# Decoder layer with experts: first expert prepared in the routing block, GpSimd constants, ringed list buffers, 4 KB norm pieces

## The reference

```
probs = softmax(x @ Wr + br);  gates, ids = top_k(probs, 2)
# each expert takes the cap = ceil(1.2 * 8192 / 8) = 1229 tokens with the highest gates
xg = x[disp_tok]                                   # (8, cap, 256)
h = silu(xg @ W1 + b1);  out = h @ W2 + b2         # hidden width 1024
y = zeros.at[disp_tok].add(out * disp_g)
x = layernorm(x + y)
```

## Time and profile before

| what | us |
|---|---|
| median of 3 runs (lowest, highest) | 1637.54 (1636.06, 1637.61) |
| the profiled execution, its own time | 1637.37 |
| its span, first to last instruction | 1635.6 |
| routing block, 970.2 to 1097.6 | 127.4 |
| experts block up to its first product, 1097.6 to 1105.4 | 7.8 |
| norm block, 1586.4 to 1635.6 | 49.2 |

### The profile page before, as it was taken

The page is one execution under the profiler, slowest core; times in us unless marked ns, Lnnn a source line. Parts: engine busy times, 40 slices in busy tenths (PEclk is TensorE's granted clock), DMA queues, the critical chain, the costliest instruction groups (busy, mean ns, idle before and its releaser), DMA issues. The chain is left out here.

```text
span 1635.6 us, 43777 instructions
## 1 busy us (share of the span) xinstructions
PE 1412.0 (86%) x17886; PEld 1188.3 (73%) x17886; DVE 1021.5 (62%) x2276; ACT 1015.4 (62%) x1555; POOL 598.8 (37%) x607
## 2 busy tenths in 40 slices
PE   7999999999999999999998560119999999999940
PEld 5777777777777777777776340119999999999940
DVE  5666666666777777777777368955455445445425
ACT  4677777777777777777766352337555456556407
POOL 2645454544433232323230000032455445545236
PEclk9999999999999999999999885559999999999975
DMA  6112122221212222222221451013443444343139
GB/s 189 33 49 62 58 61 60 60 60 60 61 60 73 79 80 78 80 67 82 70 69 45 139 165 15 1 44 82 95 104 47 97 94 95 53 99 48 22 78 355
DMA packets 128006, 129.53 MB, mean 79 GB/s; under 512 B 26496, under 2 KB 114672, under 8 KB 127808
## 3 DMA queue, kind: packets, MB, share of 16 engines
q1 hardware_dynamic: 112704, 106.24, 21.3%
q0 software_dynamic: 15104, 20.48, 7.7%
HBM read 82.53 MB, written 44.16 MB: 77 GB/s over the span
## 5 line engine op out<-in xcount | busy, mean ns | idle before, releaser
L515 ACT ACTIVATE at_pr<-at_A 128x2048 f32<-128x2048 f32 x128 | 240.7, 1880 | 147.2 <-PE at_A L335 147.2
L610 DVE TENSOR_REDUCE at_mx<-at_A 128x12 f32<-128x1536 f32 x128 | 224.6, 1754 | 56.3 <-PE at_A L300 52.7
L35 PE MATMUL ex_D<-ex_w,ex_hT 128*128 128x256 f32 (+1 forms) x1920 | 234.2, 282 | 0.3
L35 PEld LDWEIGHTS ex_D<-ex_w,ex_hT 128*128 128x128 f32 (+1 forms) x1920 | 231.0, 184 | 2.9 <-DVE ex_raw L1582 1.8
L35 PE MATMUL ex_U<-ex_xT,ex_w 128*128 128x384 f32 (+1 forms) x1152 | 224.6, 354 | 3.4 <-DVE ex_xT L1559 3.4
L1639 POOL DMA_INDIRECT total<-ex_o,ids x80 | 131.4, 1642 | 237.1 <-DVE ex_o L1587 220.1
L35 PEld LDWEIGHTS ex_U<-ex_xT,ex_w 128*128 128x128 f32 x1152 | 208.4, 190 | 12.1 <-issue 3.8
L755 POOL TENSOR_SCALAR_AFFINE_SELECT at_pr<-at_pr 128x2048 f32<-128x2048 f32 x64 | 128.5, 2007 | 205.2 <-ACT at_pr L515 205.1
L1572 DVE TENSOR_TENSOR ex_hT<-ex_h,ex_hT 128x384 fp32r<-128x384 f32 (+1 forms) x192 | 112.6, 587 | 100.2 <-ACT ex_hT L1532 90.8
L646 DVE TENSOR_TENSOR at_oT<-at_C,at_oT 128x512 fp32r<-128x512 f32 x64 | 44.2, 691 | 165.3 <-ACT at_oT L528 165.3
L335 PE MATMUL at_A<-at_qp,at_kt 32*128 32x256 f32 x2048 | 139.8, 388 | 0.0
(11 more groups left out here) (219 smaller groups left out, 2690.1 us busy)
## 6 DMA issues: line engine op xcount, KB each, us to landing
w_in<-in_w SPq DMA_DIRECT2D x16, 1024.0 KB
at_turned<-in_x_turned SPq DMA_DIRECT2D x16, 512.0 KB, 4.6
at_x<-in_x SPq DMA_DIRECT2D x16, 512.0 KB, 4.1
x<-at_y SPq DMA_DIRECT2D x32, 256.0 KB, 2.4
at_x<-x SPq DMA_DIRECT2D x16, 512.0 KB, 3.8
at_turned<-in_ctx_turned SPq DMA_DIRECT2D x16, 512.0 KB, 4.8
rows<-at_y SPq DMA_DIRECT2D x32, 256.0 KB, 2.2
total<-at_y SPq DMA_DIRECT2D x32, 256.0 KB, 3.0
```

What stands on the lines that cost most here:

```text
L35: last = nc.tensor.matmul(out, pick_l(left, a), pick_r(right, b), start=(start and n == 0), stop=(stop and n == 2))
L515: nc.scalar.activation(pr[:, k % 2].rearrange("p i n a q -> p (i n a q)"), A[:].rearrange("p i n a q -> p (i n a q)"), ACT.Exp).then_inc(e ...
L610: nc.vector.tensor_reduce(mx[:, k % 2, 0:12], A[:, 0:3].rearrange("p i n a k -> p (i n a) k"), AX, ALU.max).then_inc(max_done, 1)
```

## The change

- The shared buffers of the two blocks (inputs and rounded parts of expert 0's weights, small inputs, gathered rows, `xT`, `gate`, `ident`, the two transpose banks) are made before both.
- SP loads expert 0's small inputs in the routing block, behind its weights; the experts block's own loads of them and of `ident` go.
- ACT rounds expert 0's weights between the exponential and `low`, and chunk 0's transposes at its block end. DVE takes the weights' rests right behind `ids`, then the gates of chunk 0 and the rests of `xT`. PE transposes chunk 0 at the end of the block.
- POOL gathers two chunks (six DMAs) in the routing block; the third chunk (four) is the first thing in the experts block.
- The memsets of DVE's opening go to POOL; PE waits for them ahead of the search, DVE ahead of `gt`. `base` is no longer cleared there and `ahead` no longer copied.
- The list tables are a ring of four batches; from the fifth batch on DVE waits for the PE products of four batches earlier.
- In the norm block a partition takes four neighbouring tokens: one piece of 4 KB a load and a store.

```diff
 # route_block: ACT
             nc.scalar.activation(warm[:], dummy[:], ACT.Sign)
+            act.wait_ge(sh["w_in"], 32)
+            for src, dst, _ in weights:
+                nc.scalar.copy(dst[:, 0], src[:]).then_inc(sh["w_hi"], 1)
             act.wait_ge(split, 1)
...
+            for half in range(HALVES):
+                act.wait_ge(sh["t_full"], half + 1)
+                nc.scalar.copy(xT[:, 0, 0, half, :widths[0]], T[half][:, 0:widths[0]]).then_inc(sh["x_hi"], 1)
 # route_block: PE
             last.then_inc(pe_done, 1)
+            pe.wait_ge(cleared, 1)
             for i in range(STEPS):
...
+            pe.wait_ge(x_loaded[0], 16 * parts[0])
+            for half in range(HALVES):
+                for k, (off, n) in enumerate(tiles_of[0]):
+                    last = nc.tensor.matmul(T[half][:, off:off + n], xg[0:n, 0, k, half * P:(half + 1) * P], ident[0:n, 0:n],
+                                            start=True, stop=True, is_transpose=True)
+                last.then_inc(sh["t_full"], 1)
 # route_block: DVE
-            v.memset(xg[:, :, parts[-1] - 1, :], 0.0).then_inc(cleared, 1)
-            v.memset(ones[:], 1.0)
-            v.memset(base[:], 0.0)
-            v.memset(ones_h[:], 1.0)
-            for i in range(STEPS):
-                for j in range(3):
-                    ins = v.memset(third[:, i, j:j + 1], (j + 1) * step_of(i) - half_unit(i))
...
             dve.wait_ge(pe_done, 1)
+            dve.wait_ge(cleared, 1)
...
+                at = b % RING
+                if b >= RING:
+                    dve.wait_ge(batch_done, b - RING + 1)
...
+            for k, (src, dst, _) in enumerate(weights):
+                dve.wait_ge(sh["w_hi"], k + 1)
+                v.tensor_tensor(dst[:, 1], src[:], dst[:, 0].bitcast(FP32), ALU.subtract).then_inc(sh["w_lo"], 1)
+            dve.wait_ge(sh["small_in"], 48)
+            dve.wait_ge(x_loaded[0], 16 * parts[0])
...
 # route_block: POOL
+            nc.gpsimd.memset(ones_h[:], 1.0)
+            for i in range(STEPS):
+                for j in range(3):
+                    nc.gpsimd.memset(third[:, i, j:j + 1], (j + 1) * step_of(i) - half_unit(i))
+            for j in range(3):
+                nc.gpsimd.memset(tries[:, j:j + 1], (j + 1) * step_of(0) - half_unit(0))
+            nc.gpsimd.memset(ones[:], 1.0)
+            nc.gpsimd.memset(xg[:, :, parts[-1] - 1, :], 0.0).then_inc(cleared, 1)
             pool.wait_ge(cleared, 1)
             pool.wait_ge(gates_stored, 16)
             pool.wait_ge(ids_made, 1)
-            for s in range(AHEAD):
+            for s in range(ROUTED):
 # experts_block: POOL
+            for s in range(ROUTED, AHEAD):
+                gather(s)
 # norm_block
-                             sum_dram[g * G:(g + 1) * G, :].rearrange("(b p) n -> p b n", p=P)).then_inc(loaded[g], 16)
+                             sum_dram[g * G:(g + 1) * G, :].rearrange("(p b) n -> p b n", p=P)).then_inc(loaded[g], 16)
```

More of the change, by code:

```diff
@@ L959, in _, with route_block @@
             take(groups - 1)
-def route_block(nc, tiles, cap, logits, rows_dram, ids, first_weights, first_rows, consts):
+def route_block(nc, tiles, cap, logits, rows_dram, ids, sh, consts):
     LT = -(-cap // P)
@@ L970, in route_block @@
     PARTS = tiles // BATCH
+    _, parts, starts, widths, tiles_of = chunks_of(cap)
     DVE_TAGS = 4
+    RING = 4
     Q = 2 * tiles
@@ L1043, in route_block @@
         empty = sb("empty", [P, ROWS])
-        w1_in, w2_in, w_in = first_weights
-        xg, x_loaded = first_rows
+        xg, x_loaded, xT, chosen, gate, ident, T = (sh[name] for name in ("xg", "x_loaded", "xT", "chosen", "gate", "ident", "T"))
+        weights = ((sh["w1_in"], sh["w1"][0], "w1"), (sh["w2_in"], sh["w2"][0], "w2"))
         cleared = sem("cleared")
@@ L1092, in _ @@
                 act.wait_ge(rows_hit, b + 1)
[L1093 to L1095 removed]
+                for k in range(BATCH):
+                    t = part * BATCH + k
+                    ins = nc.scalar.activation(tagged[:, b % RING, k, :], hit_row[:, b % RING, k, :], ACT.Copy, scale=tag[:, t:t + 1])
                 ins.then_inc(tags_made, 1)
+            for half in range(HALVES):
+                act.wait_ge(sh["t_full"], half + 1)
+                nc.scalar.copy(xT[:, 0, 0, half, :widths[0]], T[half][:, 0:widths[0]]).then_inc(sh["x_hi"], 1)
         @block.tensor
@@ L1125, in _ @@
                     pe.wait_ge(dve_tags, (b + 1) // DVE_TAGS)
[L1126 to L1131, removed]
+                for k in range(BATCH):
+                    last = nc.tensor.matmul(bi[:, part, :], hit_lane[:, b % RING, k, :], tagged[:, b % RING, k, :],
+                                            start=(b % 2 == 0 and k == 0), stop=(b % 2 == 1 and k == BATCH - 1))
+                last.then_inc(batch_done, 1)
+            pe.wait_ge(x_loaded[0], 16 * parts[0])
[4 more added lines that the diff above has]
+                last.then_inc(sh["t_full"], 1)
         @block.vector
@@ L1310, in chunks_of, with shared_by_route_and_experts, sb, sem @@
     return NC, parts, starts, widths, tiles_of
-def experts_block(nc, cap, rows_dram, ids, first_weights, first_rows, sum_dram, w, consts):
+def shared_by_route_and_experts(nc, c, cap):
+    _, _, _, widths, _ = chunks_of(cap)
+    W = max(widths)
+    def sb(name, shape, dt=FP32):
+        return c.enter_context(nc.sbuf_tensor("ex_" + name, shape, dt))
+    def sem(name):
+        return c.enter_context(nc.semaphore("ex_" + name))
+    sh = {name: sem(name) for name in ("w_in", "ident_in", "small_in", "t_full", "x_hi", "x_lo", "gate_ready", "chosen_ready",
+                                       "w_hi", "w_lo")}
+    sh["x_loaded"] = [sem(f"x_loaded{i}") for i in range(XG)]
+    sh["w1_in"] = sb("w1_in", [P, HALVES, HID])
+    sh["w2_in"] = sb("w2_in", [P, HT, D])
+    sh["w1"] = [sb("w1_even", [P, 2, HALVES, HID], FP32R)]
+    sh["w2"] = [sb("w2_even", [P, 2, HT, D], FP32R)]
+    sh["b1"] = sb("b1", [P, 2, HT])
+    sh["b2"] = sb("b2", [P, 2, D])
+    sh["mask"] = sb("mask", [P, 2, E])
+    sh["xg"] = sb("xg", [P, XG, NB, D + E])
+    sh["xT"] = sb("xT", [P, 2, 2, HALVES, W], FP32R)
+    sh["chosen"] = sb("chosen", [P, NB, E])
+    sh["gate"] = sb("gate", [P, NC_CHUNKS, NB])
+    sh["ident"] = sb("ident", [P, P])
+    sh["T"] = [c.enter_context(nc.psum_tensor(f"ex_T{i}", [P, G], FP32)) for i in range(2)]
+    return sh
+def experts_block(nc, cap, rows_dram, ids, sh, sum_dram, w, consts):
     LT = -(-cap // P)
```

104 lines of the change are left out of this document (42 added, 62 removed).

## The result

The changed kernel takes 1621.92 us (median of four runs, 1621.30 to 1623.79), against 1636.80 us (1636.03 to 1637.61) before: ratio 0.9911, 95% interval 0.9894 to 0.9928. Forecast were 1622.3 us. The profiled execution took 1622.32 us, its span 1620.3 (before 1637.37 and 1635.6). What follows takes that span apart, since 15.3 us of difference that agree with 15.1 us of forecast may still be made of other parts.

A forecast was written before the change was run, and what follows sets the result against it. PE bounds the middle stage; around it, PE's waits up to its first product and DMA in the norm block were taken to bound. 11.0 + 4.1 = 15.1 us off 1637.37 gives 1622.3; range 1619.3 to 1626.8.

The forecast's parts named there:

- Parts 1 to 3: Routing block: memsets moved to POOL, weights rounded early on ACT, and the ring of list tables each change nothing, cost 0.
- Part 4: End of routing block: PE's first product moves from 1105.4 to 1094.4, gain 11.0 us, bounds 8.8 and 12.8.
- The stall of 1.7 us: End of routing block: DVE's rests of the weights hold up POOL's first two gathers, 1.7 us, bounds 0 and 4.0.
- Part 5: Experts block: third chunk's gathers start late but land before PE wants them, cost 0, 1.8 us to spare.
- Part 6: Norm block, bound by DMA: 4 KB pieces at 404 GB/s take 45.1 us, gain 4.1 us.
- the cap by ACT: Norm block: ACT's last activation plus one 512 KB store would end it at 44.1 us, capping the gain at 5.1.
- the rival built on it: Norm block: 4 KB pieces move no faster, leaving only the route's gain, 1626.4 us; chance 0.14.
- The sum: Whole kernel: 11.0 us at the routing block's end plus 4.1 in the norm block, 15.1 us off 1637.37.
- The slow rival: Routing block: small memsets on POOL at 1.04 us each delay PE's search, 31.4 us more, 1653.7; chance 0.02.

The follow-up runs named there:

- no rests: Changed kernel without DVE's two subtractions for expert 0's weights, ACT writing a plain copy in their place: 1622.01 us, ratio 0.9908.
- one chunk routed: Changed kernel with only the first chunk's three gathers in the routing block, in place of two chunks: 1624.00 us, ratio 0.9924.
- three chunks routed: Changed kernel with all ten gathers of the first three chunks in the routing block, in place of six: 1627.12 us, ratio 0.9938.

## Why the prediction was right, point by point

- *Parts 1 to 3, nothing*: right. From exponential to list it is 104.48 us in the changed kernel, 104.47 before, and 104.57 with the memsets on DVE. The margins were real: POOL was done 18 us early, ACT 5 us early, and DVE's ring waits show nowhere (PE's product of batch 4 still waits 0.98 us for DVE's tagging, as in the earlier trace rows). The ring by itself was not tried.
- *Part 4, 11.0 us*: right at 11.3, for the reasons given. The stall of 1.7 us was 1.67 (no rests), POOL came last and not DVE (one chunk routed), four gathers were worth 5.26 of the 5.28 us counted (three chunks routed). The gathers went 2.36 and 1.60 us where I had drawn 2.1 and 2.0, with nearly the same sum. The first ended 1.2 us behind DVE's first operation (about 1081.6), the second 0.9 us behind its last at 1083.80. Both are 0.1 us under the length of a free gather at that place (1.32 and 1.01 us), as if nearly all of the gather came behind the hold. The Trainium skill, "SBUF — State Buffer", section "SBUF: two separate sides", has 0.115 us behind DVE's end for the hold; for the end of the gather the measurement decides.
- *Part 5, nothing*: right. PE does not wait for chunk 2's gathers in either profile of the changed kernel, and gathering it early gains nothing. What the forecast did not look at is that the load of expert 1's weights moves with these gathers, into the us in which ACT's gaps cost PE 1.2 us in the first profile.
- *Part 6, 4.1 us*: the right mechanism, mis-sized. The rate was 412 GB/s over both directions (413 in the first us, 420 towards the end), not 404: 40.7 us for the data in place of 41.5. The median block of 43.8 us leaves 3.1 us for start and landing, not 3.6. It is also the 44.1 us of the cap by ACT that I had worked out and not taken: ACT's last activation plus 3.6 to 4.3 us in eight of twelve profiles. DMA is still full then, so the cap is met by both together. The gain is 5.3 us as a rule (49.1 to 43.8), and 3.6 in the profiled execution, whose last DMAs trickled for two us more. The Trainium skill, "DMA: Bandwidth & Descriptors", section "Specifications", has line rate from 512 B on; here 1 KB pieces ran at 366 GB/s and 4 KB ones at 412, so the rival built on it fell.
- *The sum*: 15.1 forecast, 15.3 between the spans, but part of that agreement is luck. The first 1.7 us come from code ahead of the change: the routing block starts anywhere from 968.2 to 971.5 us in these fourteen profiles. The loss of 1.2 us in the experts block was not forecast and comes and goes with the chip or the execution; that the load's new place has no part in it is not shown. Without both the profile says 11.3 + 3.6 = 14.9, and with a norm block of the usual kind 16.6; the two series of runs said 14.9 and 16.8.
- *The slow rival*, memsets of 1.04 us on POOL: off by a factor of thirty. 45 of them took 1.55 us.

## What to carry to other kernels

When a block ends with an engine's queue of DMAs, count that queue and the others apart, each with its own way out (2.5 us behind an indirect gather here, 0.5 behind DVE), and move work out of the later one until both meet; beyond that the other one decides. Look also at what waits for the work that was moved: here a weight load went with the gathers. Large DVE operations with two inputs belong into the gaps where DVE waits for PE, not beside POOL's gathers, and POOL's large operations not beside DVE's with two inputs. A span that comes out as forecast is no proof: cut it at fixed instructions and compare stretch by stretch, over several executions, before explaining one of them.

## What the runs showed that was not expected

- POOL's two subtractions (9.41 us together, against DVE's 4.49 for the same work) stopped DVE's two-input operations for 4.24 and 4.87 us, though these were only 0.69 us long.
- A stop of PE of 4.2 us cost 7.1 us, since the granted clock was 0.50 for over 5 us behind it; the waits of 0.8 to 1.1 us left it at 1.00.
- A block that is bound by DMA can end in two ways with the same code: 43.5 to 44.2 us, or 44.9 to 45.9. In the three longest of the second kind, both profiles of the changed kernel among them, a few packets (18 to 24 in the last 3 us) trickle in behind the rest. Why they are late, no run shows.
- ACT stood idle for up to 2.5 us beside a weight load in the first profile and on one chip of four, with its input ready, and not on the others. Why, no run shows.
